# Moving column loads, row loads, a result store and bias sums to other places in the queues of a two-stage transformer kernel

## The reference

```python
# first layer: graph attention over the first 20 rows of each item, in two directions
self_feat = concat(v, where(row_sum(v) == 0, 0, q)) @ W_self.T + b_self
for d in range(2):
    A = adj[:, :, :20] if d == 0 else swapaxes(adj, 1, 2)[:, :, :20]
    aff = einsum(self_feat @ Wq[d].T + bq[d], self_feat[:, :20] @ Wk[d].T + bk[d]) / sqrt(32)
    w = softmax(where(A.sum(-1) > 0, aff, NEG) + A @ w_bias + b_bias)
    output += einsum(w, self_feat[:, :20], Wout[d]) + bout[d]
x = v + relu(output)
# second layer: conditioned layer norm, 16-head attention, residual, norm again
h = gamma * (ln(x) * ln_g + ln_b) + beta        # gamma, beta from the condition vector
q, k, v = split(h @ Wqkv.T + bqkv)
out = (softmax(q @ k.T) / sqrt(512)) @ v
h1 = out @ Wp.T + bp + x
y = gamma * (ln(h1) * ln_g + ln_b) + beta + h1
```

## Time and profile before

| | us |
|---|---|
| median of 3 runs | 1318.57 |
| lowest and highest run | 1318.37, 1321.41 |
| the profiled execution, its own time | 1331.26 |
| its span | 1329.5 |
| PE busy in it | 1230.7 (93%) |
| mean granted clock of TensorE, of full speed | 0.96 |

### The profile page before, as it was taken

How to read it: one execution, slowest core, us unless ns; L and a number is a source line. 1 busy time by engine, 2 the same in 40 slices (tenths; PEclk the granted TensorE clock), 3 DMA queues, 4 the chain that set the end, 5 groups by cost and what they waited for, 6 DMA issues and landing times.

```text
span 1329.5 us, 20304 instructions
## 1 busy us (share of the span) xinstructions
PE 1230.7 (93%) x6040; PEld 840.6 (63%) x6040; DVE 887.4 (67%) x1443; ACT 633.6 (48%) x1104; POOL 885.6 (67%) x565
## 2 busy tenths in 40 slices
PE   6989979999999869899999999999999899999985
PEld 4357667777777656566676576576666566666642
DVE  2445758778878755566686686676676677677755
ACT  1323433555355535355365465465465455465551
POOL 1115457677767744676787788788687788788834
PEclk9979989999999979899899999999899999999997
DMA  9883164356435455433433433434524524534411
GB/s 337 318 293 133 33 205 181 124 210 236 149 140 199 152 175 167 112 72 96 144 84 105 140 90 104 143 87 104 145 78 110 147 77 109 147 81 110 112 35 55
DMA packets 106537, 184.11 MB, mean 138 GB/s; under 512 B 38864, under 2 KB 50448, under 8 KB 101184
## 3 DMA queue, kind: packets, MB, share of 16 engines
q1 hardware_dynamic: 96912, 157.80, 38.5%
q10 hardware_dynamic: 9520, 25.06, 6.0%
HBM read 83.92 MB, written 48.01 MB: 99 GB/s over the span
## 4 chain that ended last, share of the span: by engine, by line
PE 50%; DVE 3%; DMA 3%; SPq 2%; issue 2%; ACT 1%; ACTq 0%; POOL 0%; DVEq 0%; POOLq 0%
PE a_bank L1805 9%; PE a_bank L1854 8%; PE a_bank L107 8%; PE a_bank L1818 8%; PE a_bank L108 8%; PE a_bank L109 7%; DMA out_y<-h 2%; PE a_bank L1865 2%; SPq L1313 2%; DVE keep L1670 1%; DVE rden L1688 1%; DMA sq_stack<-sht 1%; ACT pt L1565 1%; PE a_bank L1848 1%; PE a_bank L1829 0%
## 5 line engine op out<-in xcount | busy, mean ns | idle before, releaser
L1670 DVE TENSOR_REDUCE keep<-a_bank 128x1 f32<-128x512 f32 x496 | 333.9, 674 | 232.1 <-PE a_bank L1818 229.5
L1565 ACT ACTIVATE pt<-a_bank 128x512 f32<-128x512 f32 x512 | 303.2, 598 | 377.6 <-PE a_bank L1805 329.5
L1402 POOL TENSOR_TENSOR acc<-acc,pt 128x1024 f32<-128x1024 f32 x120 | 286.7, 2389 | 25.3 <-ACT pt L1565 18.0
L1805 PE MATMUL a_bank<-sq_stack,sk_stack 98*128 98x512 f32 x512 | 222.6, 435 | 23.5 <-ACT pt L1565 11.3
L1818 PE MATMUL a_bank<-sk_stack,sq_stack 96*128 96x512 f32 x496 | 203.2, 410 | 2.9 <-DVE keep L1670 2.2
L1397 POOL TENSOR_TENSOR acc<-pt 128x1024 f32<-128x1024 f32 x60 | 143.5, 2391 | 63.8 <-PE a_bank L1865 48.3
L1805 PEld LDWEIGHTS a_bank<-sq_stack,sk_stack 98*128 98x128 f32 x512 | 99.2, 194 | 115.5 <-issue 80.3
L1086 PE MATMUL g_bank<-m,sf 128*128 128x320 f32 x512 | 140.3, 432 | 1.5 <-ACT g_bank L769 1.5
L1688 DVE RECIPROCAL rden<-a_bank 128x128 f32<-128x128 f32 x128 | 120.5, 944 | 21.0 <-PE a_bank L1848 21.0
L1854 PE MATMUL a_bank<-pt,v 128*32 128x512 f32 x1024 | 124.7, 605 | 0.0
L1086 PEld LDWEIGHTS g_bank<-m,sf 128*128 128x128 f32 x512 | 96.6, 190 | 40.7 <-issue 1.9
(11 more groups left out here) (200 smaller groups left out, 2437.9 us busy)
## 6 DMA issues: line engine op xcount, KB each, us to landing
sq_stack<-qh SPq DMA_DIRECT2D x256, 64.0 KB, 2.0
sk_stack<-kh SPq DMA_DIRECT2D x256, 64.0 KB, 2.1
m<-m_rows SPq DMA_DIRECT2D x8, 1600.0 KB, 8.1
xraw<-in_x_t SPq DMA_DIRECT2D x8, 1024.0 KB, 10.7
xn<-in_x SPq DMA_DIRECT2D x8, 1024.0 KB, 5.4
h_rows<-xn ACTq DMA_DIRECT2D x8, 1024.0 KB, 4.8
t_rows<-houth SPq DMA_DIRECT2D x8, 1024.0 KB, 4.0
t_rows<-houtl SPq DMA_DIRECT2D x8, 1024.0 KB, 6.8
```

Source lines behind the costliest of these rows:

```text
L1402: nc.gpsimd.tensor_tensor(acc[:, two, :], acc[:, two, :], pt[:, step + 1, two, :], ALU.add).then_inc(s["sum_done"], 1)
L1565: nc.scalar.activation(pt[:, i, 2 * half + k, :], bank[:, k, :], ACT.Exp).then_inc(s["exp_done"], 1)
L1670: nc.vector.reduce_max(mx[:, half, k, n:n + 1], bank[:, 2 + e % 2, :], AX).then_inc(s["emax_done"], 1)
L1805: nc.tensor.matmul(bank[:, k, :], sk[c % 2][0:3 * DH + 2, j, i * P:(i + 1) * P], sq[c % 2][0:3 * DH + 2, j, :], start=True, stop=True).the ...
```

## The change

Nothing is computed differently. Instructions stand at other places:

- `load_columns` of step 1 stands behind `load_first(2)` and no longer behind `load_m(2)`.
- In the last step of `graph`, POOL does `add_bp` for tiles 0 and 1 of item 6 ahead of its products with `rc` (L667) for tiles 1 and 2, `add_bp` for tiles 2 and 3 after the product for tile 3, and `split_lo(2)` after them. The `sk0` fill waits for `wv_lo`.
- SP and not ACT issues the store of `xn` of item 6, between `stacks(0, 0)` and `reload_x(7)`.
- In `attention`, SP issues both halves of `load_t`: part 0 ahead of the q stacks of group 1, as soon as PE's slot 6 has passed, part 1 behind `store_y(b - 1, 0)`, as soon as slot 8 has passed. ACT issues none.
- `load_last` (1 MB, item 7 alone) goes from ACT to SP, into the place of part 1.
- `load_h(b - 1, 2)` on ACT goes from slot 13 to slot 14.

```diff
@@ graph, SP: step @@
                     load_first(b + 1)
+                    if isinstance(b, int) and b == 1:
+                        load_columns()
                     sp.wait_ge(s["adj_step"], 5 * b + 5)
                     load_adj(b + 1)
...
                     load_m(b + 1)
-                if isinstance(b, int) and b == 1:
-                    load_columns()
                 if isinstance(b, int) and b < 3:
                     load_w(b - 1)
@@ graph, SP: end @@
             stacks(0, 0)
+            sp.wait_ge(s["hb_done"], 4 * B - 4)
+            sp.dma_start(d["h_rows"][B - 2], xn[:, :, :]).then_inc(s["h_stored"], 16)
             reload_x(B - 1)
@@ graph, POOL: softmax @@
                     if i >= 2:
+                        if last and i in (3, 4):
+                            add_bp(b - 1, i - 3)
                         pool.wait_ge(s["rc_done"], 4 * b + i - 1)
...
                 if last:
+                    for i in (2, 3):
+                        add_bp(b - 1, i)
                     split_lo(2)
-                    for i in range(NT):
-                        add_bp(b - 1, i)
...
             pool.wait_ge(s["sc_ready"], 4 * B)
-            pool.wait_ge(s["hb_done"], 4 * B - 4)
+            pool.wait_ge(la["wv_lo"], FC)
             nc.gpsimd.memset(sk0[3 * DH:, :, :].bitcast(F32), 1.0).then_inc(la["ones_set"], 1)
@@ graph, ACT: end @@
                     hi_rows(B - 2, i - 1)
-            store_h(B - 2)
@@ attention, SP @@
-            def load_t(b):
-
-                if not first(b):
-                    sp.wait_ge(s["k_ready"], 4 * b)
-                    sp.wait_ge(s["v_ready"], 4 * b)
+            def load_t(b, part):
+
+                G = 4 * (b - 1) + 1
+                sp.wait_ge(s["et_ready"], SLOTS * G + 2 * part + 7)
+                two = slice(2 * part, 2 * part + 2)
                 for k, dst in enumerate((hh, hl)):
-                    sp.dma_start(dst[:, 2:4, :].bitcast(F32),
-                                 d["t_rows"][ds(b, 1), k, :, 2:4, :].rearrange("o p c n -> (o p) c n")).then_inc(t_in[1], 16)
+                    sp.dma_start(dst[:, two, :].bitcast(F32),
+                                 d["t_rows"][ds(b, 1), k, :, two, :].rearrange("o p c n -> (o p) c n")).then_inc(t_in[part], 16)
+
+            def load_last(b):
+
+                sp.wait_ge(s["pv_done"], 8 * b)
+                sp.dma_start(v[:, 0], d["h_rows"][b]).then_inc(s["h4_in"], 16)
...
+                    if c == 1 and more:
+                        load_t(b + 1, 0)
                     if c < 2 or more:
                         stacks(*ahead(b, c, 2), 0, (0,))
-                    if c == 1 and more:
-                        load_t(b + 1)
                     if c == 1 and later:
                         store_y(b - 1, 0)
+                    if c == 1 and more:
+                        load_t(b + 1, 1)
+                    elif c == 1:
+                        load_last(b)
                     if c < 2 or more:
                         stacks(*ahead(b, c, 2), 0, (1,))
@@ attention, ACT (its load_t and load_last are removed) @@
-                        if slot == 9 and c == 1:
-                            load_t(b + 1) if more else load_last(b)
                         if later:
-                            if slot == 13 and c == 1:
+                            if slot == 14 and c == 1:
                                 load_h(b - 1, 2)
```

More of the change, by code:

```diff
@@ L1493, in split_hi @@
                 nc.scalar.activation(t["wph"][:, f, :], t["wp_raw"][:, f, :], ACT.Copy).then_inc(s["wp_hi"], 1)
[L1495 to L1502, removed]
             def load_h(b, i):
@@ L1515, in load_h @@
                              ).then_inc(h_in[i % 2], 16)
-            def load_last(b):
-                act.wait_ge(s["pv_done"], 8 * b)
-                act.dma_start(v[:, 0], d["h_rows"][b]).then_inc(s["h4_in"], 16)
             def project(b, c, which):
```

## The result

The changed kernel takes 1303.01 us (median of 4 runs, 1300.7 to 1303.83), the kernel before took 1318.47 in the same comparison (4 runs). The ratio is 0.9872, 95% interval 0.9851 to 0.9894. The forecast was 1273.6 with a range of 1265 to 1290: the sign was right, the size three times too large, and the time lies outside the range.

What follows compares the result with a forecast made beforehand. PE, busy 93% of the span, was taken as the bound. Gains of 11.3 - 0.5 + 4.9 + 34.2 - 2 = 47.9 us off the profiled 1331.26, cut to 45 off 1318.57, gave 1273.6 us; range 1265 to 1290.

Steps and rivals of the forecast that it cites:

- the seven windows: End of group 1 of `attention` in seven items: 34.2 us too long in all, all but 2 us to go.
- The failed step: Slot 0 of group 2: PE's remaining wait for the row of low maxima, 0.3 us on average, 2 us for seven.
- Rival 1: Row of low maxima or k stacks late at slot 0: 1290 if half the loss stays, 1303 if all; chance 0.14.
- The clock: PE after short waits at slot 0: clock stays up, as after 0.91 us, where 2.44 us slowed matmuls to 0.77.
- The base: Runs without a profile are 12.7 us shorter than the profiled execution; 3 us taken off the gain for it.
- Columns: Step 2 of `graph`: `xraw` loaded 12 us earlier, 55.32 to 44.01 us, gain 11.3, less 0.5 for `adj` in step 1.
- rival 2: Step 1 of `graph`: moved columns make `adj` late, at a cost of 4 us, giving 1277; chance 0.06.
- End of `graph`: Last step of `graph`: store of `xn` goes out earlier, gain 4.9 us, bounds 3 and 7.3; 2.4 us of wait stay.
- The store of `y`: Group 1 of `attention`: store of tile 0 lands in 2.1 us or double that, so ACT does not wait.
- rival 3: In `attention`, tile 2 of `h` late for DVE, or POOL behind: 12 us given back, 1286; chance 0.08.
- 4 and 5: In `attention`: waits move to a later group, 1317, chance 0.03; or part 0 blocks SP's queue, slower, 1325, chance 0.03.

Runs made afterwards that it cites:

- t0_act: Changed kernel with part 0 of the load of t back on ACT at slot 9: 1315.44 us, ratio 0.9922 to the kernel before.
- t1_last: Changed kernel with part 1 of the load of t issued behind the k stacks and the row of low maxima: 1287.6 us, ratio 0.9725 to the kernel before.
- before again: The kernel before, unchanged, run and profiled a second time: 1322.73 us, ratio 0.9997 to the kernel before.
- after again: The changed kernel, unchanged, run and profiled once more on another chip: 1302.76 us, ratio 0.9847 to the kernel before.
- columns alone: The kernel before with only the column loads moved: 1315.77 us, ratio 0.9939 to the kernel before.
- sums_back: Changed kernel with POOL's part of the end of `graph` undone, store on SP and early columns kept: 1306.91 us, ratio 0.9863 to the kernel before.
- `graph` edits: The kernel before with only the edits of `graph` (columns, store on SP, POOL's sums): 1303.51 us, ratio 0.9836 to the kernel before.
- t1_act: Changed kernel with part 1 of the load of t issued from ACT's queue behind exponential 12: 1297.31 us, ratio 0.9818 to the kernel before.

## Why the prediction was wrong

**Where the 45 us went.** On the profiled executions the sum fails in one term. It forecast 47.9 off 1331.26; the seven windows kept 21.7 us where 2 were allowed, 19.7 more, and 47.9 - 19.7 = 28.2, against a difference of 28.26 between the two profiled executions. That this closes so well is partly luck: `graph` gave 17.4 in place of 15.7, and `attention` outside the seven windows took 1.6 back. The rest of the miss is the step from the profiled execution to the median: it took off 3 us for the 12.7 by which the profiled before was long, and the 28.3 of the profiled pair became 15.5 between medians, 12.8 less.

**The failed step.** "What remains is a wait of 0 to 1.3 us; I take 0.3 on average, 2 us for seven." Each window kept 3.1 us, and PE waited 14.8 us at the seven slots 0, 2.1 on average. The step priced the row of low maxima at "2.1 to 3 us", hardly more than a short transfer alone, with 1 MB directly ahead of the k stacks and the row in SP's order. In the seven items slot 0 started 3.8 to 4.9 us after the row's issue. It did not price the k stacks at all: the low ones took 5.3 us in item 1 and became a wait of their own in four items. Rival 1 named both, with 0.14; what it set against itself, that less data is in flight, has the right sign (`t0_act`) but was taken for enough, while the 1 MB close ahead stayed. `t1_last` shows it by moving that 1 MB alone.

The rows of before already spoke against the store of `y` as the one cause. Item 0 stores no `y`, and yet its window was one of the long ones (29.19 us). PE's wait at its slot 0 in before, then a line of the list of PE's waits there (us in total, times, longest):

```profile
549.69 0.77 PE L1805 MATMUL a_bank<-sq_stack,sk_stack 98*128 98x512 f32 x1 [2.99 <-issue]
```

```profile
PE a_bank L1805 <- DMA sq_stack<-sht: 6.6, 2, 3.3
```

In items 4 and 5 of before the row came last, in before again in four items of seven. Item 1, whose chain was read, stands for four of the seven items at most.

**The clock.** "Such short waits seem not to bring the clock down" came from one row, 0.91 us at 1008.07, and fell. After 1.30 and 0.63 us at slot 0 of item 2, in two executions of the same kernel, the stretch behind was at 0.83 once (a mean of matmuls at full and at half clock) and at 1.00 the other time. The windows of after, then of after again (whose waits there were 1.40 and 0.61):

```profile
733.00:743.00 10.00, 9.64 (x47) 5.98 (x48) 5.20 (x11) 3.75 (x8) 5.33 (x5) 0.83 0.26 60
```

```profile
733.00:741.00 8.00, 8.00 (x48) 4.64 (x47) 5.97 (x13) 4.02 (x8) 5.53 (x6) 1.00 0.27 76
```

In after, PE's waits on issue and on the low k stacks (13.4 + 3.3 = 16.7 us, 1.9 of them at 981.84 and 1231.11, outside these windows) leave 6.9 of the 21.7 us. PE's busy time accounts for 5.4 of them (173.81 in place of 168.4), the price of the slower clock; 1.4 are waits on DVE in item 0. In before PE's busy time in the windows was 181.38, 13.0 too much, so between these two executions the clock's part fell by 7.6 us and the idle time by 4.9.

**The base.** "The runs without a profile are 12.7 us shorter, and some of that is probably in these very waits" was the right thought with too small a number. The second profile of before took 1322.53: 8.7 us less, of which 4.6 in the seven windows and 2.0 ahead of `attention`. The waits of this kernel differ between executions, so a sum made from one long execution is too large.

**Columns: right.** Step 2 came to 43.94 (forecast 44.01), with `xraw` issued at 166.38 and no wait. `adj` landed in 6.6 us against 4.5, issued at 136.30, before ACT wanted it (144.15, no wait): rival 2 did not occur. Alone, the columns moved the start of `attention` by 8.1 us and the median by 7 against before again, where the forecast was 10.8 net; step 2 by itself gave 11.1.

**End of `graph`: right in the time, less so in who gives it.** SP stored at 445.24 (forecast 446) and DVE waited 2.21 us (forecast 2.4). The term was 4.9 us. From the transposes of item 6 to the start of attention before took 75.11 us and after 69.45, so 5.7 came of it; over all executions with and without these edits it is 6.4 in the mean. `sums_back` shows that the move of the store to SP is worth little without GpSimd's part. What the term left out is the clock behind PE's wait, which came back in some executions only. The same 34 matmuls behind it kept PE busy for 9.00 us at clock 0.75 after a wait of 8.56 us (columns alone, 463 to 472 us), and for 7.20 us at 1.00 after one of 1.85 (`graph` edits, 455 to 464 us). In after, the stretch from that wait to attention got only 0.5 us shorter, 27.46 to 26.95.

**The store of `y`: right.** It landed in 2.6 us, and ACT had no wait on it. Removing one late thing left the others, 64 KB transfers that 1 MB stood close ahead of in both kernels. Of the other rivals, tile 2 of `h` took 6.2 us to land where 3.4 was assumed, and still the list of DVE's waits has a single one of 0.2 us for it (rival 3 did not occur); the ratio rules out 4 and 5.

## What to carry to other kernels

When a large transfer stands close ahead of small ones on a queue, price the small ones by rows in which such a transfer was in flight, not by the median of the page, and list all that its reader needs at that slot. Issue what is wanted first ahead of what is big: the same bytes, with 1 MB behind six stacks and a row instead of ahead of them, were worth 15 us of 1303, as much as the whole change. When a stage repeats, read the wait at the same slot in every repetition before its cause is named; one chain shows one of them. Profile the kernel a second time where its executions spread, before a sum is made on one.

## What the runs showed of the hardware

- TensorE waits of 2.7 us were followed by a granted clock of 1.00 in one place and of 0.70 in another of the same execution. In after again, 1.82 + 0.86 us at slot 0 of item 1 and 0.96 + 1.70 us at slot 0 of item 3 were followed by:

```profile
633.00:641.00 8.00, 8.00 (x47) 4.63 (x47) 5.21 (x12) 3.39 (x7) 4.09 (x5) 1.00 0.29 68
...
830.00:840.00 10.00, 9.72 (x44) 6.07 (x44) 5.28 (x11) 3.22 (x6) 3.85 (x4) 0.70 0.22 52
```

  So a wait's length alone did not set it. What does stayed open.
- Two transfers of 64 KB took 5.3 us to land with 1 MB issued 3 us ahead of them on the same queue (after, item 1). At the same place in `t1_last`, where that 1 MB came behind, they took 3.0 us.
- A second queue did not shield them: with the 1 MB issued on ACT's queue 0.6 us ahead of them they took 6.1 us (`t1_act`, item 1), and PE's waits named "issue" at the transposed scores were 15.5 us in all, against 13.4 in after.
